# A feed-forward stage on one core: gate before up, quantised values kept as 16-bit integers, no GpSimd work

## The reference, cut to what matters

```python
x = act_qdq(layernorm(x))                       # one scale for the whole tensor
up = act_qdq(x @ lpbq_dequant(w_up).T)          # 256 -> 768
gate = act_qdq(x @ lpbq_dequant(w_gate).T)
sig = fixed_qdq_u16(sigmoid(gate))              # steps of 1/65536
gate = act_qdq(gate * sig)
o = act_qdq(gate * up)
return x_in + o @ lpbq_dequant(w_down).T        # 768 -> 256
# act_qdq(x): scale = max(abs(x)) / 32767; clip(round(x / scale), -32768, 32767) * scale
# lpbq_dequant(w): the same in blocks of 32 weights, with the range -8..7
```

## Time and profile before

| | |
|---|---|
| median of 3 runs | 1731.76 us (1729.73 to 1734.66) |
| the profiled execution | 1729.73 us, its span 1727.9 us |
| feed-forward in it | 1467.9 to 1727.9 us, 260 us |
| busy over the span | TensorE 84%, VectorE 67%, ScalarE 53%, GpSimd 53% |
| chain of waits, 1640 us to the end | TensorE L1351 24.0%, VectorE L1554 12.5%, VectorE L1575 11.7% |

### The profile page before, as it was taken

One profiled execution on the slowest core, in us unless ns is written; L12 is line 12 of the kernel. 1 busy time (PEld: TensorE's weight loads), 2 busy tenths in 40 slices (PEclk: granted clock), 3 DMA queues, 4 the chain that ended last, 5 costly groups with the idle time before them and its releaser, 6 DMA issues. The chain is left out here.

```text
span 1727.9 us, 55638 instructions
## 1 busy us (share of the span) xinstructions
...
## 2 busy tenths in 40 slices
...
GB/s 172 133 119 102 129 112 144 99 98 122 119 116 131 98 114 126 112 136 98 108 128 109 144 99 99 129 117 68 29 79 90 1 0 1 55 1 1 0 0 50
DMA packets 84264, 154.94 MB, mean 90 GB/s; under 512 B 15344, under 2 KB 47864, under 8 KB 84032
## 3 DMA queue, kind: packets, MB, share of 16 engines
...
## 5 line engine op out<-in xcount | busy, mean ns | idle before, releaser
L636 DVE TENSOR_REDUCE MXP<-W_PS 128x1 f32<-128x512 f32 x768 | 499.1, 687 | 283.3 <-PE W_PS L448 283.3
L532 ACT ACTIVATE PR<-S_PS 128x1024 f32<-128x1024 f32 (+1 forms) x416 | 424.6, 1022 | 260.1 <-PE S_PS L396 252.1
L342 POOL TENSOR_TENSOR K_HI<-K,MCOL 128x512 f16<-128x512 f32 (+1 forms) x224 | 219.0, 978 | 425.3 <-ACT K L540 424.1
L344 POOL TENSOR_TENSOR K_LO<-K,K_HI 128x512 f16<-128x512 f32 (+1 forms) x224 | 291.8, 1303 | 17.6
L448 PE MATMUL W_PS<-STK,QS 105*128 105x512 f16 (+1 forms) x1024 | 269.9, 335 | 8.8 <-POOL STK L369 4.8
L396 PE MATMUL S_PS<-QS,STK 105*128 105x128 f16 (+1 forms) x3328 | 256.7, 221 | 1.0 <-DVE QS L650 1.0
L411 PEld LDWEIGHTS O_PS<-PR,V 128*17 128x17 f32 x13312 | 191.3, 98 | 78.9 <-issue 58.9
L411 PE MATMUL O_PS<-PR,V 128*17 128x64 f32 x13312 | 231.6, 220 | 7.3 <-ACT PR L532 7.2
L431 PE MATMUL W_PS<-WV_HI,CTX_HI 128*128 128x256 f16 (+1 forms) x832 | 228.4, 275 | 1.6 <-DVE WV_LO L609 1.4
L396 PEld LDWEIGHTS S_PS<-QS,STK 105*128 105x128 f16 (+1 forms) x3328 | 201.9, 99 | 44.5 <-DVE QS L650 1.1
L431 PE MATMUL W_PS<-WV_HI,CTX_LO 128*128 128x256 f16 (+1 forms) x832 | 227.9, 274 | 0.0
...
## 6 DMA issues: line engine op xcount, KB each, us to landing
...
STK<-K_HI SPq DMA_DIRECT2D x256, 128.0 KB, 2.5
STK<-K_HI SPq DMA_DIRECT2D x256, 72.1 KB, 2.1
STK<-K_LO SPq DMA_DIRECT2D x128, 128.0 KB, 2.6
STK<-K_LO SPq DMA_DIRECT2D x128, 72.1 KB, 2.1
...
```

Source lines behind the costliest of these rows:

```text
L342: pool.tensor_tensor(K_HI[:, m, lo:hi], k32, zero, ALU.add).then_inc(k_hi, 1)
L344: pool.tensor_tensor(K_LO[:, m, lo:hi], k32, K_HI[:, m, lo:hi], ALU.subtract).then_inc(k_lo, 1)
L532: nc.scalar.activation(PR[0:m, par, :], S_PS[par][0:m, :], ACT.Exp).then_inc(p_sb, 1)
L636: dve.tensor_reduce(MXP[:, j, at:at + 1], bank[:, :], AX.X, ALU.max).then_inc(mx_done, 1)
```

## The change

- Gate is projected first, then up. While up is projected, the gate's rounding, sigmoid, product and maximum run already, in orders written out for ScalarE (`UP_ACT`) and VectorE (`UP_DVE`): U moves a chunk out of PSUM, UM is its maximum, I makes gate integers, S the sigmoid, W its 16-bit unsigned steps, G the product, M its maximum, UC and US the up tensor's maximum and scale.
- Rounding is done by writing to a 16-bit integer tile (`GI`, `SI`, `XI`, `WQ`, `up_int`), in place of add and subtract.
- Weights are divided, clipped into integers and multiplied back by VectorE (`weight_round`), three passes each. Nothing is left on GpSimd in this stage.
- The input is turned before it is scaled; ScalarE normalises 6 of 16 tiles and VectorE 10. `spread` is one transpose to all partitions. The turns of up and down weights stand at gate chunks 8 and 18.
- PSUM: 5 banks for matmuls, 2 for weight turns, 1 for the maxima. The last stores are smaller.

The diff, cut: added lines and their context, and of the removed lines only GpSimd's program (the others are in the functions printed above).

```diff
+CHUNKS = FT * ROWS // CH
+RINGW = 5
+TURN = {8: 1, 18: 2}
+GATE_SCALED = 2
+UP_ACT = [
+    ("U", 0), ("U", 1), ("U", 2), ("U", 3), ("S", 0), ("U", 4), ("U", 5), ("I", 1), ("S", 1),
+    ("U", 6), ("U", 7), ("U", 8), ("U", 9), ("I", 2), ("S", 2), ("U", 10), ("U", 11), ("U", 12), ("U", 13), ("I", 3), ("S", 3),
+    ("U", 14), ("U", 15), ("U", 16), ("U", 17), ("I", 4), ("S", 4), ("U", 18), ("U", 19), ("U", 20), ("I", 5), ("S", 5),
+    ("U", 21), ("U", 22), ("U", 23),
+]
+UP_DVE = [
+    ("I", 0), ("UM", 0), ("UM", 1), ("UM", 2), ("UM", 3), ("W", 0), ("G", 0), ("M", 0), ("UM", 4), ("UM", 5),
+    ("W", 1), ("G", 1), ("M", 1), ("UM", 6), ("UM", 7), ("UM", 8), ("UM", 9), ("W", 2), ("G", 2), ("M", 2),
+    ("UM", 10), ("UM", 11), ("UM", 12), ("UM", 13), ("W", 3), ("G", 3), ("M", 3), ("UM", 14), ("UM", 15), ("UM", 16), ("UM", 17),
+    ("W", 4), ("G", 4), ("UM", 18), ("UM", 19), ("UM", 20), ("UM", 21), ("UM", 22), ("UM", 23), ("UC", 0),
+    ("W", 5), ("US", 0), ("G", 5), ("M", 4), ("M", 5),
+]
+OUT_COLS = [(0, 128), (128, 256), (256, 512), (512, 1024), (1024, 1536), (1536, 2048)]
+OUT_STORES = [(0, 4), (4, 8), (8, 12), (12, 14), (14, 15), (15, 16)]
+XN_ON_ACT = (2, 5, 7, 10, 13, 15)
...
+    UR = alloc("UR", [P, ROWS // 2 + FT * ROWS], F32)
...
+    GI = alloc("GI", [P, FT, ROWS], I16)
+    SG = alloc("SG", [P, 2, ROWS], F32)
+    SI = alloc("SI", [P, 2, ROWS], U16T)
+    WN_DOWN = alloc("WN_DOWN", [P, WCOLS], F32)
...
+    WQ = [GIF[:, 4096 + w * WCOLS:4096 + (w + 1) * WCOLS] for w in range(3)]
+    XI = GIF[:, 0:KT * ROWS].rearrange("p (k r) -> p k r", k=KT)
+    def up_int(f):
+        lo = ROWS // 2 + (f - 1) * ROWS if f else 0
+        return UR[:, lo:lo + ROWS // 2].bitcast(I16)
...
+            for e, (k, os) in enumerate(groups(w)):
+                n = WT_FIRST[w] + e
                 if n >= 2:
                     pe.wait_ge(sm["wt_lo"], n - 1)
...
+            pe.transpose(M_PS[:, 0:P], AC[:, q:q + 1].broadcast_to([P, P]), CST[:, C_ID:C_ID + P]).then_inc(sm["am_ps"], 1)
...
+        for t in range(TILES):
+            xn_done(pe, t)
+            if t % 2 == 0 and t >= 2 * RINGW:
+                pe.wait_ge(sm["xt_sb"], t // 2 - RINGW + 1)
+            for k in range(KT):
+                last = pe.transpose(W_PS[t // 2 % RINGW][:, (2 * k + t % 2) * P:(2 * k + t % 2 + 1) * P],
+                                    XN[:, t, k * P:(k + 1) * P], CST[:, C_ID:C_ID + P])
+            last.then_inc(sm["xt_ps"], 1)
...
+        spread(0)
         turn_weight(0)
         for i in range(CHUNKS):
             if i == 0:
+                pe.wait_ge(sm["xt_sb"], TILES // 2)
+            if i < 4:
+                pe.wait_ge(sm["xt_lo"], i + 1)
+            if i in (0, 12):
+                pe.wait_ge(sm["wt_lo"], WT_FIRST[0] + (2 if i == 0 else 4))
             if i in TURN:
                 turn_weight(TURN[i])
+            if i >= RINGW:
+                pe.wait_ge(sm["ga_sb"], i - RINGW + 1)
+            inner(W_PS[i % RINGW], WGT, sm["ga_ps"], i)
...
+            at = CHUNKS + i
+            if i == GATE_SCALED:
+                spread(1)
+            if i < RINGW:
+                pe.wait_ge(sm["ga_sb"], at - RINGW + 1)
             else:
+                pe.wait_ge(sm["up_sb"], i - RINGW + 1)
+            inner(W_PS[at % RINGW], WUT, sm["up_ps"], i)
...
+        pe.wait_ge(sm["wt_lo"], WT_FIRST[3])
+        pe.wait_ge(sm["up_sb"], CHUNKS)
         spread(4)
         for t in range(TILES):
+            pe.wait_ge(sm["ol"], sum(lo < (t + 1) * P for lo, _ in OUT_COLS))
+            if t >= RINGW:
+                pe.wait_ge(sm["dn_sb"], t - RINGW + 1)
...
-        for w in range(3):
-            blk = WN[:, w, :].rearrange("p (b e) -> p b e", e=WBLOCK)
-            n = WSTEPS * w
-            pool.wait_ge(sm["w_max"], 3 * w + 3)
-            def wide(t):
-                return t[:, w, :].unsqueeze(2).broadcast_to([P, NBLK, WBLOCK])
-            pool.tensor_tensor(blk, blk, wide(WI), ALU.mult).then_inc(sm["w_step"], 1)
-            pool.wait_ge(sm["w_step"], n + 1)
-            pool.tensor_scalar(blk, blk, ROUND, ROUND, ALU.add, ALU.subtract).then_inc(sm["w_step"], 1)
-            pool.wait_ge(sm["w_step"], n + 2)
-            pool.tensor_scalar(blk, blk, -W_MAX - 1, W_MAX, ALU.max, ALU.min).then_inc(sm["w_step"], 1)
-            pool.wait_ge(sm["w_step"], n + 3)
-            pool.tensor_tensor(blk, blk, wide(WS), ALU.mult).then_inc(sm["w_step"], 1)
-        for f in ON_POOL:
-            pool.wait_ge(sm["sg3"], f + 1)
-            pool.tensor_tensor(G[:, f, :], G[:, f, :], SG[:, f % 3, :], ALU.mult).then_inc(sm["g2"], 1)
-        for n, f in enumerate(OUT_ON_POOL):
-            pool.wait_ge(sm["g2i"], n + 1)
-            pool.tensor_tensor(G[:, f, :], G[:, f, :], U[:, f, :], ALU.mult).then_inc(sm["o_p"], 1)
...
+        for t in range(TILES):
+            if t in XN_ON_ACT:
+                nc.scalar.activation(XN[:, t, :], X[:, t, :], ACT.Identity, bias=VT[:, t:t + 1], scale=RS[:, t:t + 1])\
+                    .then_inc(sm["xn3a"], 1)
+            if t % 2:
+                v = t // 2
+                act.wait_ge(sm["xt_ps"], 2 * v + 2)
+                nc.scalar.activation(XT[:, :, 2 * v * P:(2 * v + 2) * P],
+                                     W_PS[v % RINGW][:, :].rearrange("p (k r) -> p k r", k=KT), ACT.Copy).then_inc(sm["xt_sb"], 1)
         keep_weight(0)
         for i in range(CHUNKS):
             if i in TURN:
                 keep_weight(TURN[i])
             act.wait_ge(sm["ga_ps"], i + 1)
+            nc.scalar.activation(unit(G, i), W_PS[i % RINGW][:, :], ACT.Copy, scale=1 / W_SCALE).then_inc(sm["ga_sb"], 1)
+        for kind, i in UP_ACT:
+            if kind == "U":
+                if i == 0:
+                    act.wait_ge(sm["w_val"], 2)
+                    act.wait_ge(sm["xt_lo"], 4)
+                act.wait_ge(sm["up_ps"], i + 1)
+                nc.scalar.activation(unit(U, i), W_PS[(CHUNKS + i) % RINGW][:, :], ACT.Copy, scale=1 / W_SCALE)\
+                    .then_inc(sm["up_sb"], 1)
+            elif kind == "I":
+                act.wait_ge(sm["sc"], 2 * SSTEPS)
+                nc.scalar.activation(GI[:, i, :], G[:, i, :], ACT.Copy, scale=INV[:, 1:2]).then_inc(sm["gia"], 1)
+            else:
+                if i == 0:
+                    act.wait_ge(sm["giv"], 1)
+                else:
+                    act.wait_ge(sm["gia"], i)
+                if i >= 2:
+                    act.wait_ge(sm["si"], i - 1)
+                nc.scalar.activation(SG[:, i % 2, :], GI[:, i, :], ACT.Sigmoid, scale=SC[:, 1:2]).then_inc(sm["sg"], 1)
+        act.wait_ge(sm["sc"], 3 * SSTEPS)
         for f in range(FT):
+            if f:
+                act.wait_ge(sm["ui"], f)
+            nc.scalar.activation(up_int(f), U[:, f, :], ACT.Copy, scale=INV[:, 2:3]).then_inc(sm["ui"], 1)
+        act.wait_ge(sm["sc"], 4 * SSTEPS)
         for f in range(FT):
+            nc.scalar.activation(GI[:, f, :], G[:, f, :], ACT.Copy, scale=INV[:, 3:4]).then_inc(sm["g2i"], 1)
+        act.wait_ge(sm["sc"], 5 * SSTEPS)
         for lo, hi in OUT_COLS:
+            nc.scalar.activation(GI[:, :, lo:hi], G[:, :, lo:hi], ACT.Copy, scale=INV[:, 4:5]).then_inc(sm["oi"], 1)
...
+        for t in range(TILES):
+            if t not in XN_ON_ACT:
+                dve.tensor_scalar(XN[:, t, :], X[:, t, :], MV[:, t, 0:1], RS[:, t:t + 1], ALU.subtract, ALU.mult).then_inc(sm["xn3"], 1)
...
+        def weight_round(w):
+            def wide(t):
+                return t[:, w, :].unsqueeze(2).broadcast_to([P, NBLK, WBLOCK])
+            blk = WN[w].rearrange("p (b e) -> p b e", e=WBLOCK)
+            ints = WQ[w].rearrange("p (b e) -> p b e", e=WBLOCK)
+            dve.wait_ge(sm["w_max"], 3 * w + 3)
+            dve.tensor_tensor(blk, blk, wide(WI), ALU.mult).then_inc(sm["w_int"], 1)
+            dve.wait_ge(sm["w_int"], w + 1)
+            dve.tensor_scalar(WQ[w], WN[w], -W_MAX - 1, W_MAX, ALU.max, ALU.min).then_inc(sm["w_clip"], 1)
+            dve.wait_ge(sm["w_clip"], w + 1)
+            dve.tensor_tensor(blk, ints, wide(WS), ALU.mult).then_inc(sm["w_val"], 1)
...
+        def scales(q):
+            n = SSTEPS * q
+            col = slice(q, q + 1)
+            dve.wait_ge(sm["const"], 1 + q)
+            dve.wait_ge(sm["am_ps"], q + 1)
+            dve.tensor_reduce(GM[:, col], M_PS[:, 0:P], AX.X, ALU.max).then_inc(sm["sc"], 1)
+            dve.wait_ge(sm["sc"], n + 1)
+            dve.tensor_scalar(SC[:, col], GM[:, col], WORTH[:, col], 1 / A_MAX, ALU.mult, ALU.mult).then_inc(sm["sc"], 1)
+            dve.wait_ge(sm["sc"], n + 2)
+            dve.tensor_scalar(SC[:, col], SC[:, col], TINY, None, ALU.max).then_inc(sm["sc"], 1)
+            dve.wait_ge(sm["sc"], n + 3)
+            dve.reciprocal(INV[:, col], SC[:, col]).then_inc(sm["sc"], 1)
+            dve.wait_ge(sm["sc"], n + 4)
+            dve.tensor_tensor(INV[:, col], INV[:, col], WORTH[:, col], ALU.mult).then_inc(sm["sc"], 1)
+            dve.wait_ge(sm["sc"], n + 5)
```

(100 more changed lines are left out.)

263 lines of the change are left out of this document (32 added, 231 removed).

## The result

The changed kernel takes 1679.26 us (median of 4 runs, 1678.86 to 1681.19); the kernel before, run beside it, 1732.31 (1729.73 to 1734.66). The ratio is 0.9696, interval 0.9679 to 0.9713: 53.0 us less by the medians. The forecast was 1685.2 us, range 1675 to 1704, so it holds. The profiled execution's span is 1676.9 us against 1727.9, 51.0 less.

A forecast was written before the change was run, and what follows sets the result against it. The last 260 us were taken as a line of VectorE work, partly contention with GpSimd, with projections inside. Engine programs laid out from 1467.9 end at 1681.3, 46.6 us off the span; 1731.8 - 46.6 = 1685.2 us, range 1675 to 1704.

The forecast's parts named there:

- the first: Rival, chance 0.14: two-source 16-bit passes stay at one element a cycle, 7.8 us more, 1693.0.
- the second: Rival, chance 0.08: every pass that touches an integer runs one element a cycle, 32.4 us more, 1717.6.
- the third: Rival, chance 0.04: the clock stays at 0.50 after the new stall through gate, 18.9 us more, 1704.1.
- the slower one: Rival, chance 0.04: VectorE's 16-bit passes on the path cost more; slower from 1.74 times, 1748.0 at twice their price.
- Part 4: Product with up: gate integers wait behind six up integers on ScalarE; a loss, 34.9 us against 31.0.
- Part 5: Output: integers, halves, then TensorE's eleven tiles in 21.5 us; first residual at 1656.4, end at 1681.3.
- Part 1: Stage start to the first matmul: it comes at 1492.4 instead of 1523.7, gain 31.3 us.
- Part 2: Gate projection: TensorE waits for the up weights' low halves, some 11.5 us of new stall; gate ends at 1546.6.
- Part 3: Up projection runs under VectorE's 53.4 us of element work; INV(3) at 1606.1 instead of 1648.9, gain 42.8 us.
- GpSimd's work: Whole stage: GpSimd's 77.5 us become three roundings (13.7 on VectorE) and six products (13.7).
- its first half: Skill's statement that offloading to GpSimd may pay where VectorE is saturated; by it the change would lose.
- The two-source price: All-16-bit difference passes: 3072 columns in 1.75 us, upper bound 3.36, which would add 7.8 us.

The follow-up runs named there:

- b1: The kernel before, with all four passes of each weight moved from GpSimd to VectorE, still in 32 bits: 1720.91 us, ratio 0.9928.
- a6: The changed kernel with the division of the up and down weights put back on GpSimd, beside chunk maxima on VectorE: 1679.27 us, ratio to before 0.9683.
- a1: The changed kernel with VectorE's low halves of the up weights moved ahead of the down weights' maxima and rounding: 1670.61 us, ratio to before 0.9634.
- a4: The changed kernel with all 24 up chunks and their maxima first, gate's element work not interleaved with them: 1689.92 us, ratio to before 0.9751.
- a2: The changed kernel with ScalarE making four up integers before INV(3) and the last two between the first gate integers: 1676.87 us, ratio to before 0.9671.
- b2: The kernel before, with the six products that GpSimd shares all on VectorE: 1733.98 us (median of 10), ratio 1.0004.
- a5: The changed kernel with the output's rounding and halves in 32 bits, as before the change: 1690.64 us, ratio to before 0.9754.

## Why the prediction was right

The forecast mechanism held step by step, and no rival's condition came true: L1546 at 1758 ns refutes the first, L1483 and L1544 (748 and 960 ns) the second, the clock at 1.00 from 1520.5 the third, and the ratio the slower one. The shifts by step (after started 0.5 us earlier than the 1467.9 that I laid the program out from):

| step | predicted | measured | difference |
|---|---|---|---|
| INV(0) | 1488.8 | 1487.4 | -1.4 |
| first gate matmul | 1492.4 | 1491.25 | -1.15 |
| low halves of up start | 1518.5 | 1516.34 | -2.2 |
| chunk 8 | 1520.2 | 1518.48 | -1.7 |
| gate's last chunk | 1546.6 | 1544.0 | -2.6 |
| I of slab 0 | 1550.9 | 1548.07 | -2.8 |
| INV(3) | 1606.1 | 1602.83 | -3.3 |
| INV(4) | 1641.0 | 1637.6 | -3.4 |
| first residual ends | 1656.4 | 1652.3 | -4.1 |
| span | 1681.3 | 1676.9 | -4.4 |

(Gate's last chunk is worked out: the down turn ends at 1536.20 in the chain, and 36 matmuls of gate remain at 0.216.) No term is off by much. Nearly all are off in one direction: 0.5 of the 4.4 is the earlier start, 0.9 the rest up to INV(0), 0.8 from there to the low halves of up, 1.1 from there to INV(3), nothing to speak of in Part 4, and 1.0 in Part 5. No run singles out a common cause.

- **Part 1** was right: the gain to the first matmul is 32.0, forecast 31.3. b1 shows that 16.5 us can be had by the weight passes alone. How the other 15.5 divide among the earlier turning, the order of the weights, the three passes instead of four and the rounding into 16 bits, no run here separates.
- **Part 2**: "and must have these low halves for the third group; behind that wait stand chunk 8 and all after it" is the row of L1281: 9.9 us idle behind WUT_LO. The terms between 1491 and 1516 came 1.0 short: 0.1 for each of three 512-row parts (1.85, not 1.95), 0.4 in the eight maxima (4.6, not 5.0), and 0.1 in each of the two roundings and two block maxima. The clock rose 3.6 us after TensorE had resumed at 1516.94, as forecast (in part by luck: in a6 it took 6.0), and cost 1.6 where I had 1.8: 0.66 in the six transposes (1.54 us; 0.88 at full clock, in the turn at 1506.15) and 0.90 in the chunks behind (13.85 for 60 matmuls, 12.95 at full rate). Undone (a1), the stall gives 8.0.
- **Part 3** was right: 54.8 us from I of slab 0 to INV(3), forecast 55.2; VectorE waits for the first sigmoid 1.53, forecast 1.3. a4 shows that the overlap gives 13.2 up to INV(3).
- **Part 4**, a loss, was right: 34.8 us, forecast 34.9. VectorE is idle 5.28 ahead of the first product; a2 gets 3.0 back.
- **Part 5** took 1.0 less than forecast: 14.7 us to the first residual's end, not 15.4, since ScalarE's six passes took 11.5 us together, forecast 12.1. The 198 matmuls took 21.8, forecast 21.5. The tail behind the last residual was 2.1, forecast 2.9; the 0.4 that I called a guess was too small.
- **GpSimd's work.** "By its first half this change would lose" is answered by b2 (ratio 1.0004 for six more products) and b1 (-9.8 us in the stage for twelve more passes). The rival's "contended L1561 stands at 1.26 times its free 2.29" misreads a mean: three of the four took 2.28 to 2.29 and one 4.73, beside GpSimd.
- **The two-source price** was the largest open term (7.8 us). The Trainium skill (VectorE: DVE Perf Modes, the perf-mode tier table) has `tensor_tensor` at 2x for bf16 operands in SBUF and at 1x for fp32. This trace agrees, for int16 and f16 in with f16 out: 1758 ns for 3072 columns against 3357 with 32-bit inputs, and 692 for 1024.
- **From span to median.** I had added 3.9 to the span; the median of after is 2.4 above its profiled span. The whole error is 5.9: 4.4 in the span, 1.5 here.

Where the gain comes from, as far as runs show it: 9.8 from the weights (b1, in the kernel before), 9.9 net from the overlap (a4), 9.9 from the 16-bit output halves (a5), nothing from the products. That is 29.6 of 49.3, if they add up: each was measured alone, one of them in the other kernel. The other 19.7 were predicted by laying the program out, and the trace has them at the forecast places, but no run isolates them.
